# Last stage: gain operands from columns of x by one-hot matmuls, with stored statistics

## The reference, cut to what matters

```python
h = _ln(x, pw_g[pathway_ids], pw_b[pathway_ids])
h = _ln(h, cp_g[compartment_ids], cp_b[compartment_ids])
t = _ln(x, tm_g[time_steps], tm_b[time_steps])
s = _ln(x, ms_g[scale_type], ms_b[scale_type])
cat = concat([w[0]*h, w[1]*t, w[2]*m, w[3]*n, w[4]*r, w[5]*s], axis=-1)   # m, n, r: x plus a vector
u = _ln(silu(cat @ int_W1 + int_b1) @ int_W2 + int_b2, int_g, int_be)
out = x + int8_matmul(u, rhs)     # tokens scaled by their absmax, rounded, clipped
```

## Time and profile before

| what | us |
|---|---|
| median of 3 runs | 1749.32 (1748.80 to 1752.99) |
| the profiled execution | 1747.66 |
| its span, first to last instruction | 1745.80 |
| TensorE busy | 1732.3 (99%) |
| VectorE busy | 1188.7 (68%) |
| ScalarE busy | 875.7 (50%) |
| GpSimd busy | 786.9 (45%) |

### The profile page before, as it was taken

The page is one execution under the profiler, slowest core; times in us unless marked ns, Lnnn a source line. Parts: engine busy times, 40 slices in busy tenths (PEclk is TensorE's granted clock), DMA queues, the critical chain, the costliest instruction groups (busy, mean ns, idle before and its releaser), DMA issues. The chain is left out here.

```text
span 1745.8 us, 23362 instructions
## 1 busy us (share of the span) xinstructions
PE 1732.3 (99%) x7935; PEld 1407.6 (81%) x7935; DVE 1188.7 (68%) x1756; ACT 875.7 (50%) x1299; POOL 786.9 (45%) x702
## 2 busy tenths in 40 slices
PE   9999999999999999999999999999999999999998
PEld 7888888888888888888888888777887788787786
DVE  8766666669989688795563335366886687587555
ACT  7655556565666565764562223243453443433433
POOL 1112221222676566564650000025577877878742
PEclk9999999999999999999999999999999999999999
DMA  6011110120243334222536568877646445544511
GB/s 208 1 49 49 48 33 15 49 73 25 103 145 128 107 111 155 97 97 106 192 118 229 186 215 284 325 244 233 218 139 179 142 162 169 160 157 148 170 38 61
DMA packets 121991, 234.36 MB, mean 134 GB/s; under 512 B 25618, under 2 KB 25874, under 8 KB 121892
## 3 DMA queue, kind: packets, MB, share of 16 engines
q1 hardware_dynamic: 91732, 157.63, 26.8%
q0 software_dynamic: 11776, 41.95, 7.3%
q10 hardware_dynamic: 18384, 33.56, 5.6%
HBM read 170.71 MB, written 58.72 MB: 131 GB/s over the span
## 5 line engine op out<-in xcount | busy, mean ns | idle before, releaser
L1081 PE MATMUL bank<-h_parts,mlp_w 128*128 128x512 f32 x2016 | 459.3, 389 | 0.6 <-ACT product_copy L1300 0.6
L1081 PEld LDWEIGHTS bank<-h_parts,mlp_w 128*128 128x128 f32 x2016 | 378.3, 188 | 80.4 <-ACT product_copy L1300 1.4
L358 PE MATMUL bank<-h_parts,gate_w 128*128 128x512 f32 x1536 | 351.1, 389 | 0.6 <-DVE h_parts L695 0.6
L358 PEld LDWEIGHTS bank<-h_parts,gate_w 128*128 128x128 f32 x1536 | 288.1, 188 | 61.9 <-issue 1.0
L2083 PE MATMUL bank<-operand_parts,int_w 128*128 128x512 f32 x1152 | 279.1, 395 | 2.5 <-ACT operand_parts L2284 1.8
L1146 PE MATMUL bank<-p_parts,mlp_out_w 128*128 128x512 f32 x1152 | 271.6, 393 | 0.3 <-DVE p_parts L1517 0.3
L1146 PEld LDWEIGHTS bank<-p_parts,mlp_out_w 128*128 128x128 f32 x1152 | 213.6, 188 | 49.2 <-issue 5.1
L2083 PEld LDWEIGHTS bank<-operand_parts,int_w 128*128 128x128 f32 x1152 | 212.5, 188 | 48.2 <-issue 3.6
L620 POOL TENSOR_TENSOR decay_sq<-decay 128x512 f32<-128x512 f32 x32 | 39.3, 1228 | 278.8 <-DVE decay L708 278.8
L1420 POOL TENSOR_TENSOR product_out<-product_out,gelu 128x512 f32<-128x512 f32 x69 | 119.7, 1756 | 97.0 <-DVE product_out L1579 96.4
L1300 ACT ACTIVATE product_copy<-bank,vec_sb 128x512 f32<-128x512 f32 x144 | 99.1, 688 | 106.1 <-PE bank L1081 105.1
(11 more groups left out here) (311 smaller groups left out, 2753.8 us busy)
## 6 DMA issues: line engine op xcount, KB each, us to landing
p_tile<-p_d ACTq DMA_DIRECT2D x96, 256.0 KB, 4.9
p_d<-product_out SPq DMA_DIRECT2D x92, 256.0 KB, 2.0
raw_mlp_w<-mlp_gate_g SPq DMA_DIRECT2D x21, 512.0 KB, 3.6
raw_mlp_w<-mlp_fc_g SPq DMA_DIRECT2D x21, 512.0 KB, 4.2
xin<-xT SPq DMA_DIRECT2D x8, 1024.0 KB, 6.8
hs_d<-u SPq DMA_DIRECT2D x8, 1024.0 KB, 5.0
hs_pair<-hs_d SPq DMA_DIRECT2D x8, 1024.0 KB, 7.8
x_columns<-xT SPq DMA_DIRECT2D x8, 1024.0 KB, 7.3
```

Of the source, the lines that this page charges most:

```text
L358: i = pe.matmul(bank[:], gw[:, w, s, k, m * P:(m + 1) * P], hr[:, q, t, k, :], start=k == 0 and n == 0, stop=k == KT - 1 and n == 2)
L1081: i = pe.matmul(bank[:], wb[g % 2][:, s, w, kk, :], hop[u % 2][o][:, t, kk, :], start=first and kk == 0 and n == 0, stop=kk == 1 and n == ...
```

## The change

- x's reciprocal deviation and shift now lie side by side (rs). For block 0 SyncE stores them to DRAM (stats_d) from their columns; for later blocks TensorE turns them in the ring place of item qt 1, ScalarE copies 8 rows of 128 out (stats_out, step 11), and SyncE stores these. SyncE then loads them back, spread to all partitions (load_stats).
- The columns of x are multiplied by the scale on VectorE (x_scaled; on GpSimd in block 0), behind each low part of x, and shifted on GpSimd (xhat_columns), which gives the centred columns xn.
- The gains of t and s come as columns: a table of gain rows in high and low parts, held at four row groups, times the one-hot matrix, one matmul of 32 rows x 512 columns an item. VectorE multiplies xn by the bank (gain_product), t into tn, s in place. ScalarE's and VectorE's high and low parts then read SBUF.
- gather_ts, t_product, scale_rows and the s product of block 0 go, with their DMAs.
- The items tt and ts move: four before step 6, four before step 10 (before: two before each of steps 6, 8, 10, 12). The bias matmuls move from behind step 8 to the front of step 10.
- The load of x columns 0 and 1 and of 2 and 3 also waits for xn_mul; x_centre waits for h_gain in place of the t and s products.

```diff
+    ITEMS_AT = {2: (4, 5), 4: (6, 7), 6: (8, 9, 10, 11), 10: (12, 13, 14, 15)}
+    GAINS_AT = {6: (8, 9), 7: (10, 11), 10: (12, 13), 11: (14, 15)}
+    BIAS_AT = 10
+    STAT_QT, STAT_AT = 1, 11
-        items.append((FRONT[o], k, ("op_low", NS, s, 0)))
+        items.append((FRONT[o], k, {"h": ("op_low", NS, s, 0), "t": ("t_prod", KT, k, 0), "s": ("s_prod", KT, k, 0)}[o]))
...
+        def store_stats(b):
+            sp.wait_ge(stat_rows_done, b)
+            sp.dma_start(stats_d[b], stat_rows[0:2 * TT, :]).then_inc(stats_stored, 16)
+
+        def load_stats(b):
+            sp.wait_ge(stats_stored, 32 + 16 * b)
+            if b:
+                sp.wait_ge(xn_add, KT * b)
+            for c in range(2):
+                sp.dma_start(spread[:, c, :], stats_d[b:b + 1, c * TT:(c + 1) * TT].rearrange("n t p -> n (t p)").partition_broadcast(P))\
+                  .then_inc(stats_loaded, 16)
...
-            for t in range(1, TT):
-                turn(t)
+            turn(1)
+            turn(2)
+            if nxt:
+                store_stats(b + 1)
+            turn(3)
+            if nxt:
+                load_stats(b + 1)
...
             while m >= 0 and items[m][0] == "qt" and prev:
+                if nxt and items[m][1] == STAT_QT:
+                    pe.wait_ge(stat_rows_done, b + 1)
+                    return
                 m -= len(ring)
             while m >= 0 and items[m][0] in ("qt", "ff") and not prev:
+                if items[m][0:2] == ("qt", STAT_QT):
+                    pe.wait_ge(stat_rows_done, 1)
+                    return
...
+        def turn_stats(b, n, prev):
+            wait_bank(b - 1, n, prev, True)
+            pe.wait_ge(S["x_rs"], 2 * (b + 1))
+            pe.transpose(bank_of[n][0:2 * TT, 0:P], rs[:, XS].rearrange("p c t -> p (c t)"), ident[:]).then_inc(stat_ps, 1)
...
+            elif kind in ("tt", "ts"):
+                if isinstance(b, int) and b == 0:
+                    pe.wait_ge(gain_done, 1)
+                pe.wait_ge(S["oh_done"], b + 1)
+                group, c = gain_of(kind, k)
+                i = pe.matmul(dst[:], gains[group, c, :], oh[group, :], start=True, stop=True, tile_position=(group.start, 0))
...
+        def stats_out(b):
+            act.wait_ge(stat_ps, b)
+            if not (isinstance(b, int) and b == 1):
+                act.wait_ge(stats_stored, 16 + 16 * b)
+            act.activation(stat_rows[0:2 * TT, :], bank("qt", STAT_QT)[0:2 * TT, 0:P], ACT.Copy).then_inc(stat_rows_done, 1)
...
                 if XF <= s + AHEAD < NS:
                     front_high(b, s + AHEAD)
+                if nxt and s == STAT_AT:
+                    stats_out(b + 1)
...
+        def xhat_columns(b, k):
+            first = isinstance(b, int) and b == 0
...
+            if first:
+                pool.tensor_tensor(by_tile(xn[:, k]), by_tile(x_columns(b, k)), spread_of(b, 0), ALU.mult).then_inc(xn_mul, 1)
+            pool.wait_ge(xn_mul, KT * b + k + 1)
+            pool.tensor_tensor(by_tile(xn[:, k]), by_tile(xn[:, k]), spread_of(b, 1), ALU.add).then_inc(xn_add, 1)
...
+        def x_scaled(b, k):
+            dve.wait_ge(S["op_low"], NS * (b - 1) + XF + KT + 2 * k + 2)
+            dve.wait_ge(stats_loaded, 32 * (b + 1))
+            dve.tensor_tensor(xn[:, k], x_columns(b, k), spread[:, 0, :], ALU.mult).then_inc(xn_mul, 1)
+
+        def gain_product(b, s):
+            o, k = steps[s]
+            dve.wait_ge(S[FRONT[o] + "_ps"], KT * b + k + 1)
+            dve.wait_ge(xn_add, KT * b + k + 1)
+            dve.tensor_tensor(source(b, s), xn[:, k], bank(FRONT[o], k)[:], ALU.mult).then_inc(S[o + "_prod"], 1)
...
-                if T_AT <= s < T_AT + TT:
-                    t_product(b, s - T_AT)
+                for later in GAINS_AT.get(s, ()):
+                    gain_product(b, later)
...
@@ first_steps (VectorE, block 0)
             split_second(0)
+            gain_product(0, 12)
+            gain_product(0, 13)
             front_low(0, 12)
             front_low(0, 13)
...
@@ end of a block on VectorE
                 for s in range(2):
                     front_low(b + 1, s)
+                    x_scaled(b + 1, s)
                 h_product(b + 1)
                 take_u(b)
                 for s in range(2, XF):
                     front_low(b + 1, s)
+                    x_scaled(b + 1, s)
```

More of the change, by code:

```diff
@@ L1832, in add_items @@
         o, k = steps[s]
-        items.append((FRONT[o], k, ("op_low", NS, s, 0)))
+        items.append((FRONT[o], k, {"h": ("op_low", NS, s, 0), "t": ("t_prod", KT, k, 0), "s": ("s_prod", KT, k, 0)}[o]))
     order = []
     for s in range(NS):
-        if s % 2 == 0 and XF <= s + AHEAD < NS:
-            for ahead in (AHEAD, AHEAD + 1):
-                add_items(s + ahead)
-                order.append(("item", len(items) - 1))
+        for later in ITEMS_AT.get(s, ()):
+            add_items(later)
+            order.append(("item", len(items) - 1))
         order.append(("main", s))
@@ L1849, in conditioned_ffn @@
     first_order = list(order)
-    for n in (0, 4):
-        at_main = next(i for i, x in enumerate(first_order) if x == ("item", n)) + 2
-        first_order.insert(at_main - 2, first_order.pop(at_main))
+    for n, count in ((0, 2), (4, 4)):
+        at_main = next(i for i, x in enumerate(first_order) if x == ("item", n)) + count
+        first_order.insert(at_main - count, first_order.pop(at_main))
     assert len(items) % len(ring) == 0
@@ L1861, in conditioned_ffn, with gain_of, source @@
     FREED = {2: 1, 3: 2, 6: 3, 7: 4}
+    def gain_of(kind, k):
+        group = (2 * k + (kind == "ts")) % 4
+        return slice(GROUP * group, GROUP * (group + 1)), k // 2
+    def source(b, s):
+        o, k = steps[s]
+        if o == "x":
+            return x_columns(b, k)
+        return {"h": lambda: bank("th", k)[:], "t": lambda: tn[:, k % 2], "s": lambda: xn[:, k]}[o]()
     def item_no(kind, k):
@@ L2069, in main @@
             o, k = steps[s]
+            if s == BIAS_AT:
+                if isinstance(b, int) and b == 0:
+                    pe.wait_ge(tab_done, 1)
+                pe.wait_ge(S["oh_done"], b + 1)
+                for m in range(KT):
+                    rows_m = slice(GROUP * m, GROUP * (m + 1))
+                    pe.matmul(A[m][:], bias_t[rows_m, :], oh[rows_m, :], start=False, stop=False, tile_position=(GROUP * m, 0))
             if isinstance(b, int) and b == 0:
@@ L2084, in main @@
                                   start=s == 0 and n == 0, stop=False)
-            if s == NS // 2:
-                if isinstance(b, int) and b == 0:
-                    pe.wait_ge(tab_done, 1)
-                pe.wait_ge(S["oh_done"], b + 1)
-                for m in range(KT):
-                    rows_m = slice(GROUP * m, GROUP * (m + 1))
-                    i = pe.matmul(A[m][:], bias_t[rows_m, :], oh[rows_m, :], start=False, stop=False,
-                                  tile_position=(GROUP * m, 0))
             i.then_inc(S["z_ps"], 1)
@@ L2383, in body @@
                     split_high(2)
+                if not prev and s == 3:
+                    act.wait_ge(gain_loaded, 16)
+                    act.activation(gain_hi[:], gain_raw[:], ACT.Copy).then_inc(gain_high, 1)
                 if not prev and s == ABS_AT:
@@ L2538, in scale_rows, with by_tile, spread_of @@
-        def scale_rows(b):
-            pool.wait_ge(S["xh_done"], TT * (b + 1))
-            pool.wait_ge(ts_rows, 16 * TT * (b + 1))
-            for t in range(TT):
-                pool.tensor_tensor(gts[t][:, 1], gts[t][:, 1], xh[:, t, :], ALU.mult).then_inc(S["s_prod"], 1)
+        def by_tile(columns):
+            return columns.rearrange("p (t q) -> p t q", t=TT)
+        def spread_of(b, c):
+            if isinstance(b, int) and b == 0:
+                return spread[:, c, :].rearrange("p (q t) -> p t q", t=TT)
+            return by_tile(spread[:, c, :])
@@ L2588, in body @@
             if prev:
-                scale_rows(b)
+                for k in range(KT):
+                    xhat_columns(b, k)
             if nxt:
@@ L2599, in body @@
                 tail_add(b - 1, [0, 1])
-            if nxt:
-                for t in range(TT):
-                    gather_ts(b + 1, t, t == 0)
             if prev:
@@ L3093, in lay_out @@
     arrays["cp_rows"] = np.repeat(c2["cp_g"], NMS, axis=0)
-    arrays["ts_rows"] = np.concatenate([np.repeat(c2["tm_g"], NMS, axis=0), np.tile(c2["ms_g"], (NCP, 1))], axis=1)
+    gain_rows = np.zeros((4, 32, 2, P), np.float32)
+    for k in range(KT):
+        part = slice(k * P, (k + 1) * P)
+        gain_rows[2 * k % 4, :2 * NCP, k // 2] = np.concatenate([c2["tm_g"][:, part]] * 2)
+        gain_rows[(2 * k + 1) % 4, 2 * NCP:NOH, k // 2] = np.concatenate([c2["ms_g"][:, part]] * 2)
+    arrays["gain_rows"] = gain_rows.reshape(P, 2 * P)
     b16 = np.stack([five(c2["cp_b"])[:NOH], five(c2["tm_b"])[:NOH], three(c2["ms_b"])[:NOH]])
```

153 lines of the change are left out of this document (86 added, 67 removed).

## The result

The changed kernel takes 1801.61 us (median of 4 runs, 1799.59 to 1806.78) against 1749.06 for the kernel before on the same chip (1746.44 to 1752.99): a ratio of 1.031, interval 1.0295 to 1.0326. The forecast was 1786 with a range of 1757 to 1800, so the sign and the mechanism held and the time lies 1.6 us above the range. The profiled execution is the slowest of the four, 1806.78 us with a span of 1804.9: 59.1 us more than the profiled one before, of which some 5 are this execution's own.

A forecast was written before the change was run, and what follows sets the result against it. TensorE, busy 99% of the span, was taken as the bound. Terms: -16.0 + 32.5 + 2.6 + 10 + 0.5 - 1.8 + 9 = +36.8 us, giving 1786 us against the median 1749.32; range 1757 to 1800.

The forecast's parts named there:

- The bank ring: Four PSUM banks taken in turn: ts3 reuses the turned statistics' bank, so TensorE waits before ts3 for ScalarE's copy.
- the copy behind the fourth q cast: ScalarE's statistics copy in step 11 stands behind q_cast(3) and front_high(13), releasing TensorE 36.7 us into blocks 1 to 5.
- the turn behind the 1 MB load: SyncE's second q transpose, issued behind load(b+2), takes 7.3 us to land and holds the fourth q cast to 35.3 us.
- (a): Rival: the waits come, but the clock does not fall or its return costs nothing; +27.8, 1777 us; chance 0.17.
- (b): Rival: turn 1 lands in 2.8 us, so block 6's floor holds in blocks 1 to 5; +9.8, 1759 us; chance 0.08.
- (d): Rival: no net change, with waits of two or three us and none in block 0; chance 0.03.
- (c): Rival: the statistics copy is no wait and the tile saving stays; 1731 us, or 1743 with VectorE late; chance 0.08.
- Waits before ts3, blocks 1 to 5: TensorE arrives at 30.2 us, is released at 36.7, and waits 6.5 us in each block, 32.5 us.
- Block 6: No load(b+2) there, so the copy is out about 32.8 us after the start; TensorE waits 2.6 us.
- Clock: TensorE's clock falls in the pauses of six blocks; each return costs 1.5 us (0 to 2.8), together +9.
- Tile saving: TensorE: 32 transposes a block go, eight gain matmuls and a statistics transpose come; 1.99 us saved a block, 16.0 together.
- Block 0: TensorE waits 10 us (4 to 13) for the statistics copy, behind VectorE's gain products, which end at 1254.4.

The follow-up runs named there:

- experiment 1: Changed kernel with ScalarE copying the turned statistics in its step 10, ahead of operand 12's high part and the fourth q cast: 1770.99 us, ratio 1.0129.
- Experiment 2: Changed kernel with SyncE issuing the second transposing DMA (turn 1) before the 1 MB load for block b+2, not behind it: 1780.91 us, ratio 1.0195.
- experiment 5: Kernel before, with one line added: in blocks 1 to 6 TensorE waits for the fourth q cast ahead of main step 10; 1774.92 us, ratio 1.0147.
- experiment 3: Changed kernel with the pause filled: 30 spare matmuls before TensorE's wait for the copy in blocks 1 to 6; 1791.35 us, ratio 1.0256.
- experiment 4: Changed kernel without GpSimd's scaling and shifting of x's columns in block 0, fills and one-column products in their place: 1797.41 us, ratio 1.0284.
- experiment 10: experiment 9 plus turn 1 ahead of the load, block 0's column tiles 2 and 3 later on GpSimd, rhs maxima ahead of gain products: 1767.19 us, ratio 1.0117.
- Experiments 7: Changed kernel with the statistics copy ahead and GpSimd's roots of the h moments ahead of the four cp_rows gathers in every block: 1765.07 us, ratio 1.0097.
- experiment 9: Kernel of experiment 7 with GpSimd's first two residual sums (u_tiles) also ahead of the cp_rows gathers: 1761.65 us, ratio 1.0078.
- experiment 11: experiment 9 with VectorE's take_u ahead of h_product at each block's end and rhs maxima ahead of gain_product(0, 8) in block 0: 1775.27 us, ratio 1.0152.
- experiment 6: Changed kernel with the copy ahead and block 0's GpSimd column operations behind block 1's two gathers, four products before four sums: 1776.00 us, ratio 1.0168.
- experiment 8: Changed kernel with the edits of experiments 1, 2, 6 and 7 together: 1773.42 us, ratio 1.0143.

## Why the prediction was right, and where it was off

**The path was right.** The bank ring, the copy behind the fourth q cast, the turn behind the 1 MB load: shown by the trace and by experiments 1, 2 and 5. Rivals (a), (b) and (d) fell. Of (c) only the price was tested: experiment 1 took the wait away, and the 1731 to 1743 that (c) gave for that case came out as 1771. Experiment 2 did the same for (b): 1781, not 1759.

**The terms**, in the profiled executions (forecast 36.8, measured 59.1):

- Waits before ts3, blocks 1 to 5: 37.2 us measured, 32.5 forecast. Release came 2.0 us later and arrival 1.1. Most of the first is the turn, which landed 8.6 to 9.2 us after its issue, outside what the earlier trace rows had shown, where the kernel before had 7.1 to 7.4.
- Block 6: 3.65 for 2.6.
- Clock: 1.67 us a pause by experiment 3, forecast 1.5; right. In blocks 4 and 5 the low clock lasted longer (0.93 over the block against 0.95 in blocks 1 to 3).
- Tile saving: 1.99 us a block forecast. In the filled kernel's block 3 (69.46 us), taking off 6.76 for the fill and 0.29 of waiting leaves 62.41 against 64.06: 1.65 saved. Eight gain matmuls took about 1.6 us, not 1.38, the statistics transpose 0.20, not 0.11, and four pairs of transposes had cost 3.2, not 3.48. Over eight blocks this is 3 us.
- **Block 0 is the step that failed**: forecast one wait of 10 us, about +9.5 with its saving and its clock; measured +20.5. The wait for the copy was only 6.64. But two more came ahead of it, 6.63 for a low part and 3.33 for rhs_peak, with a lowered clock behind the first and again behind the last two. The step said that five microseconds of row products go, 2.7 of gain products come and "I add 1": it counted VectorE's own work, and not what GpSimd's eight column operations do to VectorE's other work. For the low part that is shown, as experiment 4 took its wait away. The rows to see it by were there: products "up to 1.72 beside GpSimd" and two low parts in 4.03. I applied them to the blocks' ends and not to the opening, where GpSimd is busy for 14 us with gaps of 0.1. The wait for rhs_peak is another thing that the step left out: it stood in experiment 4 (3.4 us) and fell to 0.25 in experiment 10, where the maxima moved ahead of the gain products, so it is VectorE's order. And some 4 of the 20.5 us are the bad luck of the profiled execution; with the 81.4 and 81.1 us of experiments 2 and 3 the loss is 16 us, still 7 more than forecast.
- The remainder: low parts late by 2.7 us in blocks 1 to 6 (0.5 was counted, for blocks 6 and 7 alone), 1.1 for u_tiles at the start of block 1, block 7 2.7 shorter (forecast 2.1), and the start of the last stage 2.1 us earlier, which is chance: it lies between 1208.7 and 1214.1 over all runs.

So the forecast, 15.6 us too low against the median, missed by several terms of one sign, of which block 0 is the largest.

**The unpriced assumption** was that the rest of a block had slack. Under 7 us of pause lay the late roots, the sums beside the hidden parts, and VectorE's longer queue (50 to 54 us a block for 45). Experiments 7, 9 and 11 took these away one by one, and each time the next stood 1 to 3 us behind. That is where the tile saving goes: in block 4 of experiment 9, 2.7 us of waits stand against 1.65 saved. In block 0 no order tried brought it under 73 us.

**Left open:** why the turn behind the load takes 7 to 9 us to land when the median of all turns is 2.5, and why it took longer after the change than before; and whether block 0 can be mended with the column work on VectorE or spread further than in experiment 10. Neither was tried.

## What to carry to other kernels

When a copy is made the releaser of a PSUM bank, place it by the slowest thing ahead of it on its engine, here a DMA's landing, not by its own cost; a pause costs its length and the low clock behind it, and an old kernel with one wait added measures both. When such a wait is taken away, price the others that it had hidden before counting on the gain. And when work is moved to GpSimd, list every VectorE operation that runs beside it, the smallest too, and leave gaps in GpSimd's stream.

## What the runs showed of the hardware that was not expected

- Beside GpSimd's float32 operations of two SBUF inputs, some VectorE operations were held up whatever their size: a 128x4 tensor_scalar took 9.71 us instead of 0.17 when GpSimd had no semaphore gaps (experiment 6), 0.68 where it had them (experiment 1). Others were not: in experiment 1 bn_stats (1.87 for three) and low parts from PSUM (1.27 for two) kept their time beside them.
- Matmuls of 32 rows in four row groups overlapped only in part. In the filled kernel three of them took 0.43 us from start to the next operation, as long as the four of the bias before, which no wait cuts; four gain matmuls took about 0.93 (first group, cut by a wait into three and one) and 0.65 us (second), where a full matmul's place in a step is 0.23. So the first group had lost nearly all of its overlap.
- A wait of 2.43 us (experiment 5) and waits of 2.6 (experiment 11) were followed by steps at a lowered clock; those of 1.6 to 1.8 us in experiment 9 were followed by 5.73 us for two steps, as in full-clock blocks. The length of a wait alone does not tell: in experiment 1 the wait of 1.39 us in block 2, with waits of 0.34 and 0.24 close behind it, was followed by 3.4 us at the lower clock:

```profile
1411.00:1414.40 3.40, 3.16 (x7) 2.08 (x8) 3.04 (x3) 3.37 (x7) 2.33 (x2) 0.50 0.42 152
```

  In experiment 8 TensorE waited 2.09 us at the start of block 2 and stayed at 1.00; behind the 2.03 us at the start of block 3 the clock fell to 0.50.
